# GpSimd makes both halves of a pair's q*k products in one go, behind the scores of the pair before, and scatters behind them

## The reference, cut to what matters

```python
q = (x @ Wq + bq).reshape(B, T, 16, 8)              # T = 256, B = 32
k, v = split((x @ Wdown + bdown) @ Wup + bup)       # each (B, T, 16, 8)
q, k = apply_rope(q), apply_rope(k)
att = softmax(einsum('bthd,btgd->bthg', q, k) / sqrt(8))
out = einsum('bthg,btgd->bthd', att, v) @ Wout + bout
```

## Time and profile before

| | us |
|---|---|
| median of 3 runs | 1351.41 (1348.87 to 1352.14) |
| profiled execution, its own time | 1351.53 |
| its span, first to last instruction | 1349.4 |
| mean granted TensorE clock | 0.931 of full speed |
| POOL's products (L259), first to last | 313.5 to 679.9 |
| last scatter of the layer starts | 704.5 |
| first combine | 711.6 |

### The profile page before, as it was taken

How to read it: one execution, slowest core, us unless ns; L and a number is a source line. 1 busy time by engine, 2 the same in 40 slices (tenths; PEclk the granted TensorE clock), 3 DMA queues, 4 the chain that set the end, 5 groups by cost and what they waited for, 6 DMA issues and landing times.

```text
span 1349.4 us, 19518 instructions
## 1 busy us (share of the span) xinstructions
PE 1047.2 (78%) x6608; PEld 876.2 (65%) x6608; DVE 838.5 (62%) x1139; ACT 599.5 (44%) x1555; POOL 797.2 (59%) x613
## 2 busy tenths in 40 slices
PE   1457777675989888889862478899969999999965
PEld 1433333334877677768752468899959899988865
DVE  7948999998999999999998984011130000000028
ACT  0121111104766665666554368600006665655667
POOL 4605877776899999999870006767624444544420
PEclk9997888977999999989995799999989999999988
DMA  5472332312555455445536311399885666767647
GB/s 176 157 306 75 133 116 79 116 41 73 172 156 159 132 150 159 146 142 162 141 102 256 140 37 43 93 319 327 288 323 163 198 207 198 208 197 198 198 185 218
DMA packets 119955, 225.63 MB, mean 167 GB/s; under 512 B 16709, under 2 KB 80101, under 8 KB 117810
## 3 DMA queue, kind: packets, MB, share of 16 engines
q1 hardware_dynamic: 102164, 188.16, 45.1%
q0 software_dynamic: 17344, 35.57, 7.3%
q10 hardware_dynamic: 350, 0.67, 0.1%
HBM read 157.19 MB, written 67.14 MB: 166 GB/s over the span
## 4 chain that ended last, share of the span: by engine, by line
PE 29%; DVE 24%; POOL 21%; DMA 11%; ACT 7%; issue 6%; SPq 1%; POOLq 0%; ACTq 0%; DVEq 0%
POOL y_tok L429 10%; POOL BG L259 10%; PE ps L684 9%; PE ps L697 9%; DVE BG L998 4%; DVE BG L1030 4%; DVE BG L1039 4%; DMA FF<-sorted_x 3%; DMA TPB<-in_kpad 3%; DVE XN L899 3%; PE ps L809 2%; PE ps L811 2%; DVE stats L869 2%; PE ps L673 1%; DMA xt_d<-xT 1%
## 5 line engine op out<-in xcount | busy, mean ns | idle before, releaser
L429 POOL DMA_INDIRECT y_tok<-FF,yidx x284 | 307.7, 1083 | 209.1 <-ACT FF L497 149.6
L421 POOL DMA_INDIRECT sorted_x<-XN,idx x256 | 278.9, 1090 | 87.7 <-issue 86.3
L697 PE MATMUL ps<-FF 128*128 128x128 f32 x2272 | 277.6, 275 | 0.0
L697 PEld LDWEIGHTS ps<-FF 128*128 128x128 f32 x2272 | 265.6, 192 | 14.2 <-issue 4.3
L684 PE MATMUL ps<-FF 128*128 128x256 f32 x1136 | 274.4, 385 | 0.0
L488 ACT ACTIVATE FF<-ps,FF 128x256 f32<-128x256 f32 x568 | 230.6, 481 | 34.4 <-PE ps L684 33.8
L684 PEld LDWEIGHTS ps<-FF 128*128 128x128 f32 x1136 | 208.8, 194 | 23.3
L1160 DVE TENSOR_TENSOR BG<-BG,ps 128x512 f32<-128x512 f32 x16 | 10.6, 686 | 292.2 <-PE ps L843 292.0
L259 POOL TENSOR_TENSOR BG<-TPB 128x2048 f32<-128x2048 f32 x38 | 171.6, 4516 | 10.8 <-ACT TPB L508 10.0
L1030 DVE TENSOR_TENSOR BG<-BG,TPB 128x1024 f32<-128x1024 f32 x128 | 149.4, 1227 | 0.0
L1039 DVE TENSOR_REDUCE BG<-BG 128x256 f32<-128x4096 f32 x32 | 139.4, 4358 | 0.0
(11 more groups left out here) (187 smaller groups left out, 1689.7 us busy)
## 6 DMA issues: line engine op xcount, KB each, us to landing
FF<-in_moe SPq DMA_DIRECT2D x142, 514.0 KB
TPB<-in_kpad SPq DMA_DIRECT2D x22, 1024.0 KB, 7.8
sorted_x<-TPB SPq DMA_DIRECT2D x36, 516.0 KB, 4.0
FF<-sorted_x SPq DMA_DIRECT2D x142, 129.0 KB
FF<-in_kpad SPq DMA_DIRECT2D x10, 1024.0 KB, 7.8
BG<-y_tok SPq DMA_DIRECT2D x8, 1024.0 KB, 6.5
X<-y_tok SPq DMA_DIRECT2D x8, 1024.0 KB, 6.3
y_tok<-FF,yidx POOLq DMA_INDIRECT x284, 3.2
```

What stands on the lines that cost most here:

```text
L421: pool.indirect_dma_start(sorted_x[layer], bass.IndirectOffsetOnAxis(ap=idx[:, k, j:j + 1], axis=0), XN[:, j, :], None).then_inc(s_sc, 16)
L429: pool.indirect_dma_start(y_d[layer], bass.IndirectOffsetOnAxis(ap=yidx[:, G % 4, r:r + 1], axis=0), ys[:, G % 4, r * D:(r + 1) * D], None ...
L697: t = pe.matmul(psY[:, r * P:(r + 1) * P], hT[:, G % 2, m, r * P:(r + 1) * P], wc[:, G % 4, HID + m * D:HID + (m + 1) * D], start=False, s ...
```

## The change

POOL's step waited for `s_on` >= b-1, made the first half, scattered two tiles, waited for `s_pv` >= b, made the second half and scattered the rest. Now it waits for `s_sub` >= b+1, the scores of pair b, makes both halves, and scatters all tiles of the step.

```diff
                 late = [f - 3 for f in tiles_of(b) if f >= 3]
                 if b + 1 < NPAIR:
                     pool.wait_ge(s_qkv, 2 * (b + 1) + 2)
-                    pool.wait_ge(s_on, b - 1)
-                    qk_product(pool, b + 1, 0).then_inc(s_pp, 1)
-                for f in late[:2]:
-                    scatter_outputs(0, f)
-                if b + 1 < NPAIR:
-                    pool.wait_ge(s_pv, b)
-                    qk_product(pool, b + 1, 1).then_inc(s_pp, 1)
-                for f in late[2:]:
+                    pool.wait_ge(s_sub, b + 1)
+                    for t in range(2):
+                        qk_product(pool, b + 1, t).then_inc(s_pp, 1)
+                for f in late:
                     scatter_outputs(0, f)
             for f in range(NF - 3, NF):
                 scatter_outputs(0, f)
```

## The result

The changed kernel takes 1438.3 us (median of 4, 1434.1 to 1440.7) against 1351.8 for the kernel before (median of 4): a ratio of 1.064, 95% interval 1.061 to 1.067.

A forecast was written before the change was run, and what follows sets the result against it. POOL was taken as the bound at 19.4 us a step; the change makes it 16.2 + 8.4 = 24.6. Over 17 periods, with the first steps, that adds 88.6 to 1351.53: 1440 us, range 1424 to 1456.

The forecast's parts named there:

- The bound before: POOL's products and scatters, without gaps, set the old step of 19.4 us; DVE's apparent fullness was partly waiting.
- Who starts first: After L1016 ends, POOL's product starts at 0.08 us, before DVE asks for its first L1030 at 0.52.
- The wait of 8.4 us: DVE's four multiplies at L1030 wait 8.4 us in every steady step for POOL's pair of products.
- The step: Steady period of 24.6 us: 16.2 of DVE's work plus 8.4 of waiting; POOL idle 3 to 6 us per pair.
- How the pair holds the port: POOL's two back-to-back products take 8.94 us together and let no waiting two-input DVE instruction in between.
- rival 1: Port opens between POOL's two products and all four L1030 slip in: 1407 us; chance 5 in 100.
- ACT's chain: ACT's wait for scatter landings, then evacuation and exponential, done at about 20 of 24.6 us: 4.6 us of cover.
- PE: PE, idle for more of a step, might get a lower clock; 16.8 us busy a step leaves 7.8 of cover.
- First steps and tail: Pair 14's scores at 356.9 us, pair 31's at 774.9; last add 799.8, 88.6 later, with DVE's side just last.
- Rivals 2 and 3: Products and L1030 run side by side, 1327 us; or the new wait never acts, 1347 to 1353; each 3 in 100.
- rival 4: Scatter landings behind the pair decide through ACT's order; a period of 27 us gives 1482; chance 5 in 100.

The follow-up runs named there:

- the first experiment: The changed kernel with the pair of products waiting for `s_on` >= b-1, the old wait, instead of `s_sub`: 1366.9 us against 1347.9 for the kernel before (1.014).

## Why the prediction was right, and where it was not

- **The bound before.** POOL's list without gaps was the bound. Moving a quarter of the products off it gained 24 us, which it could not have if DVE's own work or ACT had set the step.
- **Who starts first.** Forecast: the product 0.08 us behind L1016, the first multiply at 0.52. Measured: 504.90 and 505.26 behind 504.75, so 0.15 and 0.51. Right.
- **The wait of 8.4 us.** The group takes 12.94 for 4.62: 8.3. Right.
- **The step.** 24.56 us for 24.6, the same for 3 and 4 tiles, with POOL idle 2.85 to 5.37 us for the forecast's 3 to 6. Right. L1012 and L1038 at their minima: right.
- **How the pair holds the port.** This step failed. I took it from one row, L1042 at 315.79, that a waiting instruction stays out over both halves; the steady step lets one multiply in. The row itself was read rightly, and it repeats (the same instruction takes 6.88 us there in the changed kernel), but it stands behind a scatter and does not carry over to pairs that start after idle time. The sum stood all the same, because it rests on order alone, as the forecast says under rival 1: if one multiply goes in between, the second half is later by its length and the three others wait for that. 8.94 + 4.62 is spent in either order, and the error only shows in the pair's length (9.95, not 8.94). The claim gave the forecast its high chance, and should have been priced from both sides; the version in which it matters, all four going in, would have been 1407.
- **ACT's chain.** Forecast with 4.6 us of cover left. DVE waits for ACT nowhere in 360 to 750, though ACT waits 134.8 us. The exponential is done at 523.44, and DVE takes it at 529.23: 5.8 us of cover. Right; with the pair 5 us later (behind `s_pv`) that cover is gone and 0.9 us a step appears, so it was not far off.
- **PE.** Busy 18.2 us a step (288.3 over 15.9 steps) at a granted clock of 0.85 for 0.98; the clock fell, and the cover of 6 us took it.
- **First steps and tail.** Pair 14's scores are ready at 357.34 (forecast 356.9), pair 31's at 774.99 (774.9), the last add ends at 799.89 (799.8), combine 88.8 us later (88.6). That DVE's side is the last one was wrong, by little: DVE waits 0.48 us for the loads behind the last scatters before the first combine. POOL's last scatter ends at 794.1 for the forecast's 792: the last pair ends at 760.5 for 759.4, and the scatter at 785.71 waits 2.10 us for ACT, which the forecast did not have.
- **Total.** 1440 forecast; 1440.7 in the profiled execution, 1438.3 in the median, range 1424 to 1456. Rivals 2 and 3 would show clean multiplies, rival 4 idle time of DVE in front of L1021; neither is there.

The Trainium skill's rule (SBUF — State Buffer, "Who interferes with whom"), that the one who issues first holds the shared pair for the whole instruction, agrees with the steady step better than my reading of the first pair did: one multiply got in between two products in 18 of 19 pairs. The pairs behind a scatter do not fit it: the L1012 of 357.88 was issued during the first half, before the second half started at 360.4, and was kept out over both. The same section says that a DVE instruction with two SBUF inputs is kept out by a GpSimd instruction that reads SBUF and not by one that only writes; the run with constants shows it, 4.62 us beside the writes for 12.94 beside the products.

## What to carry to other kernels

Before a wait is moved, write down what the other engine runs at the moment at which the new semaphore fires: here the wait fired 0.5 us ahead of the only long stretch of DVE with two SBUF inputs. GpSimd's products then add nearly their whole length to that stretch (8.3 us for a pair of 8.94, 4.0 for a half of 4.5). The same pair beside reductions (the first experiment) costs DVE 4.0 us a step, all in L1012, and the kernel 19 us instead of 87. A busy engine whose instructions vary in length at one shape, as L1016 did (0.69 to 4.37 us), may be waiting; a part of the work moved there from the engine that is really full gained 24 us here.

## What was not expected of the hardware

- Two products of POOL in a row let exactly one waiting DVE instruction in between them if POOL had been idle before (pairs of 9.95 us), and none if they followed a scatter without a pause (8.92 to 9.00 us), although in the first experiment an L1012 had been waiting since 2 us after the start of such a pair (7.53 us for its 0.69). An idle time of 0.46 us was enough, and a tiny write between the scatter and the pair changed nothing. A wait for the first half's end opened the door there too (2.44 us for 6.90). The cause is open.
- A scatter of POOL beside DVE's multiplies takes 1.27 to 1.96 us for its 0.96, while no product runs. In the changed kernel the first two scatters behind a pair, beside the last multiplies, take 1.80 and 1.93.
